# Values of the later batches folded one head at a time, and a new order of the first steps, in a gated cross-attention block

## The reference

```python
def bitlinear(x, w):
    return act_quant(x) @ weight_quant(w).T      # 127 levels a row; w in {-1, 0, 1} / scale
...
q = (x @ Wq).reshape(B, Sq, h, d).transpose(0, 2, 1, 3)
k = (context @ Wk).reshape(B, -1, h, d).transpose(0, 2, 1, 3)
v = (context @ Wv).reshape(B, -1, h, d).transpose(0, 2, 1, 3)
attn = jax.nn.softmax(jnp.einsum('bhid,bhjd->bhij', q, k) * scale, axis=-1)
out = jnp.einsum('bhij,bhjd->bhid', attn, v).transpose(0, 2, 1, 3).reshape(B, Sq, h * d)
... # out @ Wo + bo
g = bitlinear(x, w_gate)
u = bitlinear(x, w_up)
h = jnp.square(jax.nn.relu(g)) * u               # then bitlinear(h, w_down)
...
x = x + jnp.tanh(g_xattn[0]) * _L0_xattn_ref(_layernorm(x, axis=-1), ctx_768, ...)
x = x + jnp.tanh(g_ffn[0]) * _L0_ffn_ref(_layernorm(x, axis=-1), ...)
```

## Time and profile before

| what | us |
|---|---|
| median of 3 runs | 1191.43 (1191.32 to 1191.89) |
| the profiled execution, whole | 1190.42 |
| span of its trace | 1188.6 |
| TensorE busy | 1174.0 (99%) |
| VectorE busy | 1033.9 (87%) |
| ScalarE busy | 869.2 (73%) |
| GpSimd busy | 307.2 (26%) |
| first `gate_up` matmul starts at | 85.13 |

### The profile page before, as it was taken

The page is one execution under the profiler, slowest core; times in us unless marked ns, Lnnn a source line. Parts: engine busy times, 40 slices in busy tenths (PEclk is TensorE's granted clock), DMA queues, the critical chain, the costliest instruction groups (busy, mean ns, idle before and its releaser), DMA issues.

```text
span 1188.6 us, 18855 instructions
## 1 busy us (share of the span) xinstructions
PE 1174.0 (99%) x5867; PEld 744.8 (63%) x5867; DVE 1033.9 (87%) x2124; ACT 869.2 (73%) x929; POOL 307.2 (26%) x313
## 2 busy tenths in 40 slices
PE   9989999999999999999999999999999999999998
PEld 7656656665665666566566656666665666666554
DVE  4989898888988888888998888889899888988887
ACT  5877777776887677677877767776787777677764
POOL 3222222222442222222442222222244222222200
DMA  9793554444444464444444464443444444444333
GB/s 356 262 297 77 156 147 100 98 111 97 97 112 102 126 158 114 96 108 97 101 100 101 115 179 108 98 110 93 101 113 101 100 97 110 97 101 108 84 65 76
DMA packets 286485, 144.71 MB, mean 122 GB/s; under 512 B 254586, under 2 KB 255226, under 8 KB 283889
## 3 DMA queue, kind: packets, MB, share of 16 engines
q1 hardware_dynamic: 286445, 144.32, 47.7%
q10 hardware_dynamic: 4, 0.00, 0.0%
HBM read 57.86 MB, written 24.35 MB: 69 GB/s over the span
## 4 chain that ended last, share of the span: by engine, by line
PE 86%; DVE 7%; ACT 3%; issue 2%; DMA 1%; POOL 0%; DVEq 0%; ACTq 0%; POOLq 0%
PE gu_ps L1084 34%; PE o_ps L1048 17%; PE y_ps L1098 17%; PE s_ps L66 17%; DVE half_max L1330 1%; DVE staged L1324 1%; DMA staged<-in_wd_t 1%; PE gu_ps L1148 1%; PE gu_ps L1208 1%; DMA a_scr<-a_spare 0%; DVE w_up L1484 0%; DVE staged L1456 0%; ACT staged L778 0%; DVE w_down L1484 0%; ACT x_marked L854 0%
## 5 line engine op out<-in xcount | busy, mean ns | idle before, releaser
L1084 PE MATMUL gu_ps<-w_up,xq_t 128*128 128x512 bf16 x1024 | 241.9, 379 | 1.9 <-DVE staged L1324 1.9
L1084 PE MATMUL gu_ps<-w_gate,xq_t 128*128 128x512 bf16 x1016 | 240.9, 380 | 1.3 <-DMA xq_t<-xq 1.2
L1098 PE MATMUL y_ps<-w_down,hq_t 128*128 128x512 bf16 x1008 | 227.8, 379 | 0.0
L1048 PE MATMUL o_ps<-v_sb,pt_high 128*128 128x512 f32 (+1 forms) x640 | 212.8, 413 | 0.9 <-DVE pt_low L1313 0.9
L1324 DVE TENSOR_TENSOR staged<-staged,gu_ps 128x1024 f32<-128x1024 f32 x128 | 155.6, 1216 | 53.5 <-ACT staged L784 53.5
L66 PE MATMUL s_ps<-a_sb,xf_high 128*128 128x308 f32 x1024 | 187.4, 305 | 0.0
L1084 PEld LDWEIGHTS gu_ps<-w_up,xq_t 128*128 128x128 bf16 x1024 | 100.0, 98 | 123.6 <-DVE staged L1324 3.8
L645 POOL TENSOR_TENSOR rstd<-var_eps,neg_half 128x1 f32<-128x1 f32 x128 | 96.4, 753 | 307.1 <-DVE var_eps L1289 274.6
L824 ACT ACTIVATE staged<-staged,h_scale 128x1024 f32<-128x1024 f32 x126 | 137.9, 1142 | 48.9 <-DVE h_scale L1344 48.9
L1098 PEld LDWEIGHTS y_ps<-w_down,hq_t 128*128 128x128 bf16 x1008 | 98.8, 98 | 118.8
L778 ACT ACTIVATE staged<-gu_ps 128x1024 f32<-128x1024 f32 x127 | 128.9, 1015 | 52.4 <-PE gu_ps L1084 52.0
(11 more groups left out here) (146 smaller groups left out, 1438.8 us busy)
## 6 DMA issues: line engine op xcount, KB each, us to landing
xf_sb<-in_x_feat SPq DMA_DIRECT2D x64, 256.0 KB, 2.6
x_sb<-in_x_tok SPq DMA_DIRECT2D x64, 256.0 KB, 2.9
y<-staged SPq DMA_DIRECT2D x63, 256.0 KB, 2.0
staged<-in_wg_t SPq DMA_DIRECT2D x4, 1024.0 KB, 9.5
staged<-in_wd_t SPq DMA_DIRECT2D x4, 1024.0 KB, 7.6
folded<-a_scr SPq DMA_DIRECT2D x3, 1232.0 KB, 5.6
v_scr<-x SPq DMA_DIRECT2D x12, 256.0 KB
folded<-v_scr SPq DMA_DIRECT2D x3, 1024.0 KB, 5.1
```

Of the source, the lines that this page charges most:

```text
L1048: last = nc.tensor.matmul(o_ps[:, :], pt[0:rows, P * c:P * (c + 1)], v_sb[0:rows, v, c, :], start=(c == 0 and pt is pt_high and v == 0), s ...
L1084: last = nc.tensor.matmul(target[:, q, :], xq_t[:, s.par(0), c, :], w[:, c, cols], start=(c == 0), stop=(c == DC - 1))
L1098: last = nc.tensor.matmul(y_ps[:, :], hq_t[:, c, :], w_down[:, c, :], start=(c == 0), stop=(c == FC - 1))
```

## The change

**Values.** Batch 0 is folded as before. Batches 1 to 3 are folded together, head by head: `fold_later_values(k)` takes head k // 2 and one of two halves (116 and 115 rows) of the 231 keys of the three batches. It reads the head's 64 rows of `v_t` directly, so it is one matmul on 64 rows of the array, and `place_values` runs once instead of four times. That is 16 matmuls where there were 24, and 16 copies where there were 15. A half spans two batches, so it is stored by two DMAs (32 in all, 15 before), to a `v_scr` that is now laid out row by row.

**Places.** Seven SBUF places serve the 16 parts (`V_PLACE`), with six semaphores for their stores: three tiles of `x1`, `bo_sb`, `probs_t`, and two pieces of `k_pairs` for the last two.

**Loads.** All eight gate and up pieces are asked for at the start, with no wait between them; the second tile's features and the x tiles come after them. The first down piece goes to `v_pairs`, as soon as the values of batch 0 are folded.

**Sharing.** VectorE measures six pieces (four before) and scales six (seven before); ScalarE measures six (eight before) and scales six (five before). The lists of all engines up to step 0 are written in a new order. On VectorE `input_stats(start, 0)` now stands before the first low parts of the keys, and `split_bias` between them.

**Step 0.** VectorE starts with `add_attention` and `input_scale`; the statistics of tile 3 come after `unmark_input`, both halves of `hidden_half` come earlier, and `ternary(2, 0)` has moved into the step. ScalarE has a `first_step`, in which `mark_input` stands before `join_probs`.

```diff
-V_OUT_RING = 3
+V_PLACE = [0, 1, 2, 3, 4, 0, 1, 2, 3, 4, 0, 1, 2, 3, 5, 6]
+V_STORE = [min(n, 5) for n in V_PLACE]
+FIRST_ROWS = ((BATCH - 1) * KEYS + 1) // 2
...
+def head_part(k):
+
+    h, s = divmod(k, 2)
+    return h, KEYS + FIRST_ROWS * s, FIRST_ROWS - s
...
+                def store_later_values(k):
+                    at = KEYS * head_part(k)[0]
+                    sp.wait_ge(vo_taken, k + 1)
+                    for b, j, n, r in part_runs(k):
+                        sp.dma_start(v_scr[b, at + j:at + j + n, :].rearrange("p (q n) -> p q n", q=HP),
+                                     v_slots[V_PLACE[k]][r:r + n, :, :]).then_inc(v_stored[V_STORE[k]], 16)
...
+                def first_step(s):
+                    relu_half(s, 0)
+                    square_half(s, 0)
+                    scale(2, 2)
+                    part_probs(s, 2)
+                    scale(2, 3)
+                    mark_input(s, 1)
+                    join_probs(s, 2)
+                    probs_high(s, 2)
+                    high_part(s, 4)
+                    relu_half(s, 1)
+                    square_half(s, 1)
+                    exponentials(s, 3)
...
+                def fold_later_values(k):
+
+                    h, first, rows = head_part(k)
+                    if k < V_RING:
+
+                        pe.wait_ge(v_split_done, KC + k - V_RING + 1)
+                    else:
+                        pe.wait_ge(vo_taken, k - V_RING + 1)
+                    own = slice(HEAD * (h % 2), HEAD * (h % 2 + 1))
+                    nc.tensor.matmul(value_slots[(KC + k) % V_RING][0:rows, :], v_t[own, h // 2, first:first + rows], wo_sb[own, h // 2, :],
+                                     start=True, stop=True, tile_position=(HEAD * (h % 2), 0)).then_inc(vo_done, 1)
...
                 def first_step(s):
-                    input_stats(s, 3)
-                    hidden_half(s, 0)
                     add_attention(s, 1)
                     input_scale(s, 1)
+                    hidden_half(s, 0)
+                    unmark_input(s, 1)
+                    input_stats(s, 3)
                     top_scores(s, 3)
-                    unmark_input(s, 1)
+                    hidden_half(s, 1)
                     shift_scores(s, 3)
+                    probs_low(s, 2)
+                    ternary(2, 0, w_down)
                     top_half(s, 0)
                     ternary(2, 2, w_down)
-                    hidden_half(s, 1)
-                    probs_low(s, 2)
                     ternary(2, 3, w_down)
```

442 lines of the change are left out of this document (227 added, 215 removed).

## The result

| kernel | median, us | ratio to before (95%) |
|---|---|---|
| before | 1191.34 (10 runs) | |
| changed | 1195.38 (1194.28 to 1197.39, 10 runs) | 1.0039 (1.0030 to 1.0047) |

The change makes the kernel 4.0 us slower. The forecast was +1.6 us, the range 1187.5 to 1197.0: the time lies inside the range, but on the slower side of what can be told from no change, where I had put 0.30.

What follows compares the result with a forecast made beforehand. VectorE's work before the steady steps was taken as the bound: opening 26.6, work 76.9, idle 4.4, lengthening 2.2 sum to 110.1 against 108.5, +1.6 us, so 1193.0 us; range 1187.5 to 1197.0.

Steps and rivals of the forecast that it cites:

- VectorE's account: VectorE's time from its first measure of an up piece to tile 0's rounded hidden values; claimed to set the start.
- opens: VectorE's first measure of an up piece, forecast at 26.6 us, 0.4 later than before.
- work: VectorE's operations between opening and close at their clean durations, forecast to go from 74.3 to 76.9 us.
- lengthening beside GpSimd: Extra time of VectorE's operations while GpSimd works: four meetings at 0.55 each, 2.2 us, 3.0 before.
- idle: VectorE's waits between opening and close, forecast at 4.4 us, of which 2.8 before the second hidden_half; 5.0 before.
- closes: VectorE's rounded hidden values of tile 0, forecast at 110.1 us, 108.50 before; the end moves with it.
- Sharing: On VectorE, two more measures and one scale fewer, +3.2 us; the bias's low part done before the opening, -0.6.
- Loads: Weight pieces arrive earlier, but VectorE's first measure is for piece (1,3), one later: 26.6 us from 0.40 MB/us.
- Rival 4: Each of GpSimd's four operations blocks VectorE in full: 2.8 us more, 1195.8 us; chance 0.10.
- The bracket in step 0: VectorE idle 2.8 us before the second hidden_half, since ScalarE's second relu stands behind joining, which waits for a transpose.
- rival 3: ScalarE's joining waits over 3.5 us after the transpose's issue, behind 17 more store issues; 1195.0 at 5.5; chance 0.20.
- the wait in step 1: TensorE starts the first gate_up some 6 us earlier, then waits 4 to 6 us for step 1's first hidden_half.

Runs made afterwards that it cites:

- The second profile: The changed kernel run and profiled once more, as it is ("after, again" in the table): profiled execution 1194.47 us, median 1196.09 us, ratio 1.0037.
- the one with the old step: The changed kernel plus four filling matmuls, with step 0 in the order of the kernel before on VectorE and ScalarE's mark_input behind join_probs: 1194.19 us, ratio 1.0021.

## Why the prediction was right, and where it was wrong

**That VectorE's account sets the start: right.** From the close to the end of the span it is 1080.1 us before, and 1080.0 to 1081.0 in thirteen profiles of the changed kernel and its variants, whether the clock was halved behind the close or not, and with 4.9 us less work on TensorE. 0.5 of the spread is a wait for a transpose in the last step (1174.12 in the profile after), which some profiles have and others don't.

**The terms.** The second profile, at 1194.47, is 0.9 below the median, as that of the kernel before is below its own, and its half clock before the close (69 to 73 us) held up no row of VectorE, so I compare with it too:

| term, us | before | forecast | after | after, again |
|---|---|---|---|---|
| opens | 26.23 | 26.6 | 27.05 | 26.68 |
| work | 74.3 | 76.9 | 76.3 | 76.0 |
| lengthening beside GpSimd | 3.0 | 2.2 | 3.7 | 3.7 |
| idle | 5.0 | 4.4 | 7.4 | 5.5 |
| closes | 108.50 | 110.1 | 114.46 | 111.89 |
| close to end of span | 1080.1 | as before | 1080.7 | 1080.7 |

*Sharing (+2.6 of work).* It came to 1.7 to 2.0. The direction and most of the sum are right, as a price on the path it is not: undoing 2.2 of it left the account as long as it was (84.5).

*Loads.* Opening forecast at 26.6, measured at 26.68 to 28.56 in the ten profiles in which VectorE measures (1,3) first, each time behind a wait for that piece. I worked it out from one transfer rate and gave it no spread; it had almost two microseconds.

*Lengthening (2.2, measured 3.7).* This term failed by 1.5. I counted four meetings at 0.55. There were five (rows at 39.61, 49.84, 59.69, 71.45 and 89.73, together 3.7, so 0.74 each); I had left out the `normalise` of tile 2 beside `ternary(2, 1)`. Rival 4 was on the right side and too large: it had 2.8 more, 1.5 came, of which 0.9 is the fifth meeting. None of the five reached 1.25.

*The bracket in step 0 (2.8, measured 2.34 to 3.75).* Place and releaser were right, and that the size was near is partly luck. I derived it from one chain, over the transpose (its terms, 85.6, 3.5 and 5.3, give 94.4 and not 94.2, so 0.2 more); the runs showed two. The mark of the input alone makes 2.4, and the transpose adds what it is late. I took 3.5 us from its issue to the joining, from the earlier trace rows; in the second profile it was 4.7 (89.28 to 93.94), in the one with the old step 6.3. That is rival 3, with the point I gave for it (4.3 us). Of its mechanism this much is shown: the stores took 1.25 us each and not 0.34, and with them moved the wait was zero. But the trace of the kernel before already had a slow one, issued at 87.83 with 2.15 us of issue and 5.0 to its landing; ScalarE was busy there, and no bracket showed it. I took the row at 113.01 in its place.

*TensorE.* The folds by head were not slow and not on the path, as forecast. The first `gate_up` was forecast for 78 to 80 and began at 83 in the profiled execution, at 80.1 in the second; the wait in step 1 was forecast at 4 to 6 and was 3.68 and 3.66. The half clock was in no part of the forecast: in the profile in which it struck near 80 us there are 3.1 us of waits for TensorE (2.09 and 1.00), and the bracket behind them is 1.4 shorter than in the other (2.34 for 3.75).

**The sum of the errors**, on the second profile: work -0.9, lengthening +1.5, idle +1.1, opening and the last step's wait +0.7, together +2.4: 1.6 forecast, 4.0 measured. That the time lies inside the range owes something to its width: it was drawn for rivals 3 and 4 one at a time. The mechanism was right, and two slower rivals, which I took for alternatives, came true together, each in part. What stays open is the rest of the opening's spread, why the planes landed 4.6 us after a short issue in the second profile, and how often TensorE's clock falls at one idle stretch: one profile a kernel can't tell.

## What to carry to other kernels

Where one engine's account sets the end, check at each meeting point how late the others are: an operation taken off the account is worth only what they leave, here nothing of 2.2 us. Stores that nobody waits for can bring the issuing engine late to a transfer that somebody waits for; put them behind the last critical issue. And let reductions run beside GpSimd's operations, and the multiplications that write bf16 in its pauses.
